# The low part of a stacked operand, formed by GpSimd in two instructions and not by VectorE in one

## The chip, the cores and the metric

One core of a Trainium2 chip runs the whole program. The metric is the device time of one execution in microseconds; a kernel's time is the median of several executions. A core has five engines that run side by side, each with a queue of its own in program order: TensorE (PE, with its weight loads as PEld), VectorE (DVE), ScalarE (ACT), GpSimd (POOL) and SyncE (SP), which issues the transfers here. They wait for each other by semaphores. TensorE's clock has two levels, 1.2 and 2.4 GHz; the profile's granted clock is the share of the higher one.

## The reference

Two layers over 8 sequences of 256 tokens with 1024 features. Cut to what matters:

```python
x = x + L0_ffn(L0_cond(x, w0, itok14), gamma, beta, w1, b1, w3, b3)   # int8 fake-quant feed-forward
# second layer
base  = einsum('bsi,oi->bso', x, weight) + bias
low   = einsum('bsi,bri->bsr', x, lora_a[adapter])                    # rank 16
z     = base + scale[adapter] * einsum('bsr,bor->bso', low, lora_b[adapter])
n     = z * rsqrt(mean(z*z) + eps)
H_res = sinkhorn_50(n @ W_res.T + base_res)      # a 4x4 matrix per token
H_pre, H_post = softmax(n @ W_pre.T + ...), softmax(n @ W_post.T + ...)
x_pre = sum_n(z_streams[n] * H_pre[n])           # 4 streams of 256
out   = x + einsum(H_res, z_streams) + (x_pre @ W_branch) * H_post
```

The products of the second layer run with float32 operands split in two: a rounded high part and a low part, the difference between the full value and the high part. A product is then hi x hi + hi x lo + lo x hi.

## The kernel before

`adaln_ffn` has one block for each engine, and each block is the engine's instructions in program order, so the order on an engine is the order of the Python code. The first layer runs over the sequences `s` and ends, on TensorE, near 460 us. The second layer then runs step `b` = 0 to 7, one sequence of two token tiles (`t` = 0, 1) per step. `b` = 0 has most of its base products woven into the end of the first layer.

**A step on TensorE** (L1042): the base products of tile 0, half 0 (`base`, 24 matmuls L1003), the rank-16 products `low_and_heads` (L991), the transposes of the previous sequence's gathered stream (`branch_transposes`, L1027, which wait on `xp_step` for each tile), base of tile 0, half 1, then `low_rank` (L1011) for both halves, which adds the low-rank term and the bias and waits for `ls_done` and for `e_lo`, then `branch` (L1037), which waits for `xpT_lo`, and the same for tile 1, with the heads and the transposes of the next step's input between.

**The stacked operand.** `low_rank` is one matmul with the stack `ls` (rows 0 to 31 and 32 to 63 the high part of `low`, rows 64 to 95 its low part) against the stack `es` of the adapter's B matrix, the head columns and the bias: `es` holds the high part in rows 0 to 31 and 64 to 95 and the low part in rows 32 to 63. SyncE loads the raw rows three times into `estage` (96 x 1048, float32) and the adapter's scale into `e_scale`; these nine loads wait for the `e_lo` of the step before (`load_lora`, L367). ScalarE writes `es[0:96] = estage * e_scale`, rounded (`stack_hi`, L670, semaphore `e_hi`). VectorE then overwrites rows 32 to 63 with `estage * e_scale - es` in one instruction (L1346, in `lo_stacks`, semaphore `e_lo`), and, in the same function, forms the low part of `ls` (L1349, `ls_done`).

**A step on VectorE** (L1527): `lo_stacks(b)`; `lo_xp(b-1)` (L1417, the low part of the transposed gathered stream); two shares of Sinkhorn iterations; `lo_xT` (L1323) for the next step's tile 0; a third share; `lo_xT` for tile 1; `softmaxes(b)`; `gather(b)`, which forms `xp` of both tiles in two L1399 and six L1405 (`xp = y * hp + xp`); a fourth share. The shares (L1495, L1499, L1502: multiply, reduce, reciprocal) exist in steps 4 to 7 alone. Ahead of step 4 stand `gate_rest` and `sinkhorn_start(0)`, in which VectorE and ScalarE alternate. The iterations of the second half of the tokens follow after step 7.

**A step on ScalarE** (L728): `stack_hi(b)`, the three copies of `evac_ll` (L674 to L676, `f_done`), `evac_xp(b-1)`, the evacuations of `y`, `lora_hi(b+1)` (L664), the high part of the next input, and last `head_root` and `head_exp` of the softmaxes.

**GpSimd** works for the first layer (additions L480 and subtractions L474) and clears the stacks; in the second layer it has one instruction a step, `av_lo` (L496).

Of the kernel before, what the change touches and what calls it, by code (L numbers as in the profile page):

```python
# [9 lines left out]
ALU = mybir.AluOpType  # L10
# [13 lines left out]
def adaln_ffn(nc, x_tok, x_tr, cond_w, ids_cond, ids_lora, gamma, beta, w1, b1, w3, b3, base_w, base_w_nat,  # L24
              lora_a, lora_bt, lora_b_nat, bias_row, bias_col, scaling, head_w, head_base, gate, branch_w, out):
    NB, _, NTOK, D = x_tok.shape
    KC = D // P
    PAIRS = KC // 2
# [26 lines left out]
    def wait(eng, sem, n):  # L55

        if isinstance(n, int) and n <= 0:
            return
        eng.wait_ge(sem, n)

    with ExitStack() as ctx:
# [12 lines left out]
        def sb(name, shape, dt):  # L74
            return sb_in(rest, name, shape, dt)

        def sem(name):
            return ctx.enter_context(nc.semaphore(name))
# [51 lines left out]
        estage = sb("estage", [LZ, D + NH], F32)  # L130
        es = sb("es", [P, D + NH], F32R)
        e_scale = sb("e_scale", [LZ, 1], F32)
# [61 lines left out]

        x1n_ld = [sem(f"x1n_ld{t}") for t in range(NTOK)]
        xt_done, xh_done, xl_done = sem("xt_done"), sem("xh_done"), sem("xl_done")
        a_ld, a_hi, a_lo, e_ld, e_hi, e_lo = sem("a_ld"), sem("a_hi"), sem("a_lo"), sem("e_ld"), sem("e_hi"), sem("e_lo")
        ll_done, f_done, ls_done = sem("ll_done"), sem("f_done"), sem("ls_done")
        l1_done, lg_done, y_ev, ss_done = sem("l1_done"), sem("lg_done"), sem("y_ev"), sem("ss_done")
        hd_step, hd_sqrt, hd_exp, xp_step = sem("hd_step"), sem("hd_sqrt"), sem("hd_exp"), sem("xp_step")  # L200
# [264 lines left out]
        @block.gpsimd  # L465
        def _(pool):
            nc.gpsimd.memset(ident[:, :], 0.0).then_inc(id_zero, 1)
            pool.wait_ge(id_zero, 1)
            nc.gpsimd.affine_select(out=ident[:, :], in_=ident[:, :], compare_op=ALU.not_equal, fill=1.0,
                                    base=0, pattern=[[-1, P]], channel_multiplier=1).then_inc(id_set, 1)  # L470

            def split_lo(pr):
                pool.wait_ge(whi_done, pr + 1)
                nc.gpsimd.tensor_tensor(w_lo[pr][:, :, :], w_raw[pr][:, :, :], w_hi[pr][:, :, :],  # L474
                                        ALU.subtract).then_inc(wlo_done, 1)

            def add_b3(s):
                pool.wait_ge(xr_ld, 16 * (s + 1))
                for t in range(NTOK):
                    nc.gpsimd.tensor_tensor(xres[:, t, :], xres[:, t, :], vecs[:, V_B3, :], ALU.add).then_inc(xb3_done, 1)  # L480

            pool.wait_ge(bias_ld, 16 * 2)
            for s in range(HALF - 2):
                add_b3(s)
            split_lo(0)
            split_lo(1)
            add_b3(HALF - 2)
            split_lo(2)
            split_lo(3)
            for s in range(HALF - 1, NB):  # L490
                add_b3(s)


            def lora_lo(b):
                pool.wait_ge(a_hi, b + 1)
                nc.gpsimd.tensor_tensor(av_lo[:, :, 0:RANK], a_st[:, :, :], av_hi[:, :, 0:RANK],  # L496
                                        ALU.subtract).then_inc(a_lo, 1)

            pool.wait_ge(l0_pair, PAIRS * NB)
            pool.wait_ge(m1_done, 4 * NB)  # L500
            nc.gpsimd.memset(estage[:, :], 0.0)
            nc.gpsimd.memset(e_scale[:, :], 1.0)
            nc.gpsimd.memset(es[:, :].bitcast(F32), 0.0)
            nc.gpsimd.memset(ls[:, :].bitcast(F32), 0.0).then_inc(b_zero, 1)
            pool.wait_ge(b_zero, 1)
            nc.gpsimd.memset(ls[0:32, :].bitcast(F32), 1.0)
            nc.gpsimd.memset(ls[32:64, :].bitcast(F32), 1.0).then_inc(b_set, 1)
            for b in range(NB):
                lora_lo(b)


        @block.scalar
# [667 lines left out]
        def _(dve):  # L1180
# [161 lines left out]


            def lo_stacks(b):
                dve.wait_ge(e_hi, b + 1)
                nc.vector.scalar_tensor_tensor(out=es[32:64, :], in0=estage[32:64, :], scalar=e_scale[32:64, 0:1],  # L1346
                                               in1=es[32:64, :], op0=ALU.mult, op1=ALU.subtract).then_inc(e_lo, 1)
                dve.wait_ge(f_done, b + 1)
                nc.vector.tensor_tensor(ls[LO:LO + RANK, :], PS[0:RANK, LL_BANK, 0:S], ls[0:RANK, :],  # L1349
                                        ALU.subtract).then_inc(ls_done, 1)  # L1350
# [176 lines left out]
            def step_b(b, first=False, last=False, sink=False):  # L1527

                def share(i):
                    if sink:  # L1530
                        n = B_ITERS // 4
                        iterations(0, (b - NB // 2) * B_ITERS + i * n, n)

                lo_stacks(b)
                if not first:
                    lo_xp(b - 1)
                share(0)
                share(1)
                if not last:
                    lo_xT(b + 1, 0)  # L1540
                share(2)
                if not last:
                    lo_xT(b + 1, 1)
                softmaxes(b)
                if not last:
                    gather(b)
                share(3)
# [121 lines left out]
```

## Time and profile before

| | before |
|---|---|
| runs | 820.75, 821.10, 825.47 us; median 821.1 |
| the profiled execution | 823.01 us, span 821.2 us |
| PE busy | 740.1 us, 90% of the span |
| PEld busy | 470.2 us, 57% |
| DVE busy | 528.1 us, 64% |
| ACT busy | 349.4 us, 43% |
| POOL busy | 69.2 us, 8%, 40 instructions |
| chain that ended last | PE 64%, DVE 14%, ACT 11%, DMA 6%, issue 4% |
| granted TensorE clock, mean | 0.965 |

Busy times of different engines overlap. The chain of work that ended last is followed back from the last instruction, at each step to what released it. The idle time in square brackets of a timeline row is what the engine stood still just before the instruction, and behind the arrow is what ended it. Rows of a timeline with x2 or x6 are several instructions, merged; their length is from the start of the first to the end of the last.

### The profile page before, as it was taken

To read this page: it belongs to the slowest core of one execution; us is meant where nothing else is said; L and a number is where in the kernel's file an instruction comes from. 1 tells how busy PE (TensorE), PEld (TensorE's weight loads), DVE (VectorE), ACT (ScalarE), POOL (GpSimd) and SP (SyncE) were. 2 spreads that over 40 slices of the span, in tenths; PEclk is the share of its full clock that TensorE was granted. 3 is DMA by queue.
4 is the path that set the end of the run, shared out by engine and by line. 5 is a ranking of instruction groups with operands and counts; after the bars stand their busy time and mean duration, and the time that the engine had idled before them with its cause. 6 is when DMAs were issued, how large, how long until landed. Compare 5 with 4: busy or idle time off the path is not lost.

```text
span 821.2 us, 9900 instructions
## 1 busy us (share of the span) xinstructions
PE 740.1 (90%) x3112; PEld 470.2 (57%) x3112; DVE 528.1 (64%) x1911; ACT 349.4 (43%) x660; POOL 69.2 (8%) x40
## 2 busy tenths in 40 slices
PE   5977989997989999999999799999899997599927
PEld 2543444353434444444565588888778775367626
DVE  4568254415485756558476445134988988999985
ACT  1234332322443324243455544344454243499714
POOL 0002000201432202002203000000000000000000
PEclk9997999999999999999999999999999999799968
DMA  8978964312545655351303231231230327666406
GB/s 322 405 161 337 242 215 157 137 52 77 208 163 225 262 163 187 103 202 42 113 27 133 86 116 47 70 116 46 71 114 4 116 76 256 217 227 205 150 1 204
DMA packets 54134, 124.31 MB, mean 151 GB/s; under 512 B 7999, under 2 KB 33727, under 8 KB 48450
## 3 DMA queue, kind: packets, MB, share of 16 engines
q1 hardware_dynamic: 52786, 120.94, 42.4%
q10 hardware_dynamic: 1296, 2.74, 1.3%
q8 instruction: 25, 0.41, 0.2%
q14 instruction: 27, 0.22, 0.1%
HBM read 98.47 MB, written 25.19 MB: 151 GB/s over the span
## 4 chain that ended last, share of the span: by engine, by line
PE 64%; DVE 14%; ACT 11%; DMA 6%; issue 4%; SPq 0%; ACTq 0%; DVEq 0%
PE PS L834 21%; PE PS L894 14%; PE PS L1003 13%; PE PS L883 3%; DMA stage<-w_dram 3%; PE PS L1155 2%; DVE xp L1405 2%; PE PS L1115 2%; PE PS L925 2%; ACT blk L783 2%; DMA out_dram<-mr 2%; PE PS L1109 1%; PE PS L1037 1%; ACT qT L561 1%; ACT L690 1%
## 5 line engine op out<-in xcount | busy, mean ns | idle before, releaser
L834 PE MATMUL PS<-w_raw,x_raw 128*128 128x512 f32 x512 | 227.8, 598 | 10.9 <-DMA w_raw<-cond_w_dram 9.6
L834 PEld LDWEIGHTS PS<-w_raw,x_raw 128*128 128x128 f32 x512 | 96.0, 192 | 120.1 <-issue 119.6
L1003 PE MATMUL PS<-w_hi,xT_hi 128*128 128x512 f32 x256 | 102.5, 401 | 0.0
L1003 PE MATMUL PS<-w_hi,xT_lo 128*128 128x512 f32 x256 | 100.1, 391 | 0.0
L1003 PE MATMUL PS<-w_lo,xT_hi 128*128 128x512 f32 x256 | 99.8, 390 | 0.0
L561 ACT ACTIVATE qT<-PS,round_c 128x512 bf16<-128x512 f32 x64 | 40.4, 679 | 76.2 <-PE PS L883 76.2
L1255 DVE SCALAR_TENSOR_TENSOR gbuf<-PS,lnst,vecs 128x512 f32<-128x512 f32 x32 | 23.9, 750 | 75.7 <-PE PS L894 75.7
L480 POOL TENSOR_TENSOR xres<-xres,vecs 128x1024 f32<-128x1024 f32 x16 | 44.0, 2774 | 315.5 <-DMA xres<-x_tok_dram 315.5
L894 PE MATMUL PS<-w3q,qT 128*128 128x512 bf16 x256 | 61.3, 395 | 9.9 <-ACT qT L561 9.9
L1499 DVE TENSOR_REDUCE ksum<-kprod 128x16 f32<-128x64 f32 x392 | 66.4, 211 | 0.0
L894 PE MATMUL PS<-w1q,qT 128*128 128x512 bf16 x256 | 59.6, 387 | 2.2 <-ACT qT L561 2.2
L1323 DVE TENSOR_TENSOR xT_lo<-PS,xT_hi 128x512 fp32r<-128x512 f32 x32 | 20.5, 682 | 62.9 <-ACT xT_hi L621 62.8
L1003 PEld LDWEIGHTS PS<-w_hi,xT_lo 128*128 128x128 f32 x256 | 48.0, 188 | 10.4
L1003 PEld LDWEIGHTS PS<-w_lo,xT_hi 128*128 128x128 f32 x256 | 48.2, 188 | 9.1
L1003 PEld LDWEIGHTS PS<-w_hi,xT_hi 128*128 128x128 f32 x256 | 48.1, 188 | 8.9
L894 PEld LDWEIGHTS PS<-w3q,qT 128*128 128x128 bf16 x256 | 25.1, 101 | 47.6 <-ACT qT L561 14.5
L682 ACT ACTIVATE y<-PS 128x512 f32<-128x512 f32 x32 | 18.2, 598 | 74.5 <-PE PS L1011 74.5
L894 PEld LDWEIGHTS PS<-w1q,qT 128*128 128x128 bf16 x256 | 25.1, 99 | 37.4 <-issue 8.7
L1282 DVE SCALAR_TENSOR_TENSOR x1buf<-PS,q2st,vecs 128x512 f32<-128x512 f32 x32 | 23.6, 750 | 33.0 <-PE PS L894 33.0
L540 ACT ACTIVATE hbuf<-hbuf,round_c,lnst 128x1024 f32<-128x1024 f32 x16 | 19.9, 1241 | 47.9 <-DVE lnst L1242 47.9
L1265 DVE TENSOR_REDUCE q2st<-gbuf 128x1 f32<-128x1024 f32 x16 | 19.5, 1219 | 30.1 <-ACT gbuf L545 30.1
L1502 DVE RECIPROCAL ka<-ksum 128x16 f32<-128x16 f32 x196 | 36.3, 227 | 0.0
(178 smaller groups left out, 1171.4 us busy)
## 6 DMA issues: line engine op xcount, KB each, us to landing
w_raw<-cond_w_dram SPq DMA_DIRECT2D x32, 1024.0 KB, 5.6
x_raw<-x_tr_dram SPq DMA_DIRECT2D x32, 256.0 KB, 6.3
stage<-w_dram SPq DMA_DIRECT2D x16, 512.0 KB, 13.4
xres<-x_tok_dram SPq DMA_DIRECT2D x8, 1024.0 KB, 9.2
x_scratch<-x1buf SPq DMA_DIRECT2D x16, 512.0 KB, 6.3
x1n<-x_scratch SPq DMA_DIRECT2D x16, 512.0 KB, 5.7
y_scratch<-y SPq DMA_DIRECT2D x16, 512.0 KB, 3.4
stage<-base_w_nat_dram SPq DMA_DIRECT2D x8, 512.0 KB, 9.7
```

The costliest lines, as they stand in the source:

```text
L480: nc.gpsimd.tensor_tensor(xres[:, t, :], xres[:, t, :], vecs[:, V_B3, :], ALU.add).then_inc(xb3_done, 1)
L540: nc.scalar.activation(hbuf[t][:, :], hbuf[t][:, :], ACT.Identity, bias=round_c[:, 0:1], scale=lnst[:, t, 9:10]).then_inc(q1_done, 1)
L561: nc.scalar.activation(qT[t][:, 4 * h:4 * h + 4, :], PS[:, T_BANK + h, :].rearrange("p (c n) -> p c n", c=4), ACT.Identity, bias=round_c[: ...
L834: mm = pe.matmul(PS[:, 2 * t + h, :], x_raw[pr][:, c, t * P:(t + 1) * P], w_raw[pr][:, c, h * H2:(h + 1) * H2], start=(pr == 0 and c == 0) ...
L883: tr = pe.transpose(PS[:, T_BANK + h, c * P:(c + 1) * P], src[t][:, (4 * h + c) * P:(4 * h + c + 1) * P], ident[:, :])
L894: mm = pe.matmul(PS[:, O_BANK + h, :], qT[t][:, c, :], wq[:, c, h * H2:(h + 1) * H2], start=(c == 0), stop=(c == KC - 1))
L1003: pe.matmul(PS[:, 2 * t + h, :], xx[:, c, t * P:(t + 1) * P], ws[c // 2][:, c % 2, h * H2:(h + 1) * H2], start=(c == 0 and xx is xT_hi and ...
L1255: nc.vector.scalar_tensor_tensor(out=g[:, h * H2:(h + 1) * H2], in0=PS[:, O_BANK + h, :], scalar=lnst[:, t, 8:9], in1=vecs[:, V_SW1, h * H ...
L1282: nc.vector.scalar_tensor_tensor(out=x1buf[t][:, h * H2:(h + 1) * H2], in0=PS[:, O_BANK + h, :], scalar=q2st[:, t, 1:2], in1=vecs[:, V_SW3 ...
L1323: nc.vector.tensor_tensor(xT_lo[:, 4 * h:4 * h + 4, t * P:(t + 1) * P], PS[:, T_BANK + h, :].rearrange("p (c n) -> p c n", c=4), xT_hi[:, ...
L1499: nc.vector.tensor_reduce(ksum[i][:, :, :], kprod[i][:, :, :, :], AX.X, ALU.add).then_inc(k_step[i], 1)
L1502: nc.vector.reciprocal(new[i][:, :, :], ksum[i][:, :, :]).then_inc(k_step[i], 1)
```

## The change

VectorE's L1346 goes. GpSimd gets a function `stack_lo(b)` with two instructions over rows 32 to 63: `estage = estage * e_scale`, in place, and, after a semaphore of its own, `es = estage - es`, which signals `e_lo` as L1346 did. GpSimd runs `stack_lo(b)` between `lora_lo(b)` and `lora_lo(b+1)`, and `lora_lo` gets a wait for the `e_lo` of the step before. The other engines wait for the same semaphores as before.

```diff
-        a_ld, a_hi, a_lo, e_ld, e_hi, e_lo = sem("a_ld"), sem("a_hi"), sem("a_lo"), sem("e_ld"), sem("e_hi"), sem("e_lo")
+        a_ld, a_hi, a_lo, e_ld, e_hi, e_scaled, e_lo = sem("a_ld"), sem("a_hi"), sem("a_lo"), sem("e_ld"), sem("e_hi"), sem("e_scaled"), sem("e_lo")
...
             def lora_lo(b):
+                wait(pool, e_lo, b)
                 pool.wait_ge(a_hi, b + 1)
...
+            def stack_lo(b):
+                pool.wait_ge(a_lo, b + 1)
+                pool.wait_ge(e_hi, b + 1)
+                nc.gpsimd.tensor_scalar(estage[32:64, :], estage[32:64, :], e_scale[32:64, 0:1], None, ALU.mult).then_inc(e_scaled, 1)
+                pool.wait_ge(e_scaled, b + 1)
+                nc.gpsimd.tensor_tensor(es[32:64, :], estage[32:64, :], es[32:64, :], ALU.subtract).then_inc(e_lo, 1)
+
+            lora_lo(0)
             for b in range(NB):
-                lora_lo(b)
+                stack_lo(b)
+                if b + 1 < NB:
+                    lora_lo(b + 1)
...
             def lo_stacks(b):
-                dve.wait_ge(e_hi, b + 1)
-                nc.vector.scalar_tensor_tensor(out=es[32:64, :], in0=estage[32:64, :], scalar=e_scale[32:64, 0:1],
-                                               in1=es[32:64, :], op0=ALU.mult, op1=ALU.subtract).then_inc(e_lo, 1)
                 dve.wait_ge(f_done, b + 1)
```

GpSimd's queue at the end of its memsets, where the second layer starts, before:

```order
L504 MEMSET ls 128x256
L506 MEMSET ls 32x256
L507 MEMSET ls 32x256
L496 TENSOR_TENSOR av_lo<-a_st,av_hi 128x8x16 x8
L61 UNCONDITIONAL_BRANCH
```

and after the change, where the code stands one line further down:

```order
L505 MEMSET ls 128x256
L507 MEMSET ls 32x256
L508 MEMSET ls 32x256
L497 TENSOR_TENSOR av_lo<-a_st,av_hi 128x8x16
L512 TENSOR_SCALAR estage<-estage,e_scale 32x1048
L514 TENSOR_TENSOR es<-estage,es 32x1048
L497 TENSOR_TENSOR av_lo<-a_st,av_hi 128x8x16
L512 TENSOR_SCALAR estage<-estage,e_scale 32x1048
L514 TENSOR_TENSOR es<-estage,es 32x1048
```

The eight `av_lo` stood in a row and now have a scaling and a subtraction behind each of them.

VectorE's queue where step 5 ends its predecessor's fourth share and begins, before:

```order
L1499 TENSOR_REDUCE ksum<-kprod 128x16 x2
L1502 RECIPROCAL kb<-ksum 128x16 x2
L1346 SCALAR_TENSOR_TENSOR es<-estage,e_scale,es 32x1048
L1349 TENSOR_TENSOR ls<-PS,ls 16x256
L1417 TENSOR_TENSOR xpT_lo<-PS,xpT_hi 128x512
L1495 TENSOR_TENSOR kprod<-kmat,kb 128x64 x2
```

and after it (L1510 was L1502, L1357 was L1349, L1425 was L1417, L1503 was L1495):

```order
L1507 TENSOR_REDUCE ksum<-kprod 128x16 x2
L1510 RECIPROCAL kb<-ksum 128x16 x2
L1357 TENSOR_TENSOR ls<-PS,ls 16x256
L1425 TENSOR_TENSOR xpT_lo<-PS,xpT_hi 128x512
L1503 TENSOR_TENSOR kprod<-kmat,kb 128x64 x2
```

The low part of `ls` follows directly on the last reciprocal; nothing else moved on VectorE.

## Rows read from the trace of the kernel before

**Rows 1.** Chain that ended last, in time: start us, length us, engine, out, line
```profile
477.22 1.99 DVE xp L1405 x5
...
480.09 5.48 PE PS L1003 x24
...
611.46 1.30 DVE es L1346
...
782.89 12.42 issue
```

**Rows 2.** Timelines of step 5, ScalarE, VectorE, TensorE: start us, us, instruction, idle before
```profile
602.80 1.16 ACT L670 ACTIVATE es<-estage,e_scale 96x1048 fp32r<-96x1048 f32 x1
...
604.09 2.46 DVE L1405 SCALAR_TENSOR_TENSOR xp<-y,hp,xp 128x256 f32<-128x256 f32 x6
...
611.46 1.30 DVE L1346 SCALAR_TENSOR_TENSOR es<-estage,e_scale,es 32x1048 fp32r<-32x1048 f32 x1
...
612.79 0.41 DVE L1349 TENSOR_TENSOR ls<-PS,ls 16x256 fp32r<-16x256 f32 x1
...
613.24 0.69 DVE L1417 TENSOR_TENSOR xpT_lo<-PS,xpT_hi 128x512 fp32r<-128x512 f32 x1
...
606.21 0.83 PE L1027 MATMUL PS<-ident,xp 128*128 128x128 f32 x4 [0.45 <-DVE xp L1405]
...
612.13 0.39 PE L1003 MATMUL PS<-w_hi,xT_lo 128*128 128x512 f32 x1
...
613.26 0.72 PE L1011 MATMUL PS<-es,ls 128*128 128x512 f32 x2 [0.74 <-DVE ls L1349]
...
614.08 0.35 PE L1037 MATMUL PS<-wb_hi,xpT_hi 128*128 128x256 f32 x1
```

**Rows 3.** Instructions that touch es: duration ns min/median/max, first and last start
```profile
L1346 DVE SCALAR_TENSOR_TENSOR es<-estage,e_scale,es x8: 1298/1298/1300, 462.1 to 675.7; 32x1048 fp32r<-32x1048 f32 x8
```

**Rows 4.** Timelines of GpSimd and VectorE, two places of the first layer
```profile
248.48 4.50 POOL L474 TENSOR_TENSOR w_lo<-w_raw,w_hi 128x2048 fp32r<-128x2048 f32 x1 [10.85 <-ACT w_hi L517]
...
248.62 5.45 DVE L1287 TENSOR_TENSOR x1buf<-x1buf,xres 128x1024 f32<-128x1024 f32 x1
...
73.91 5.64 POOL L480 TENSOR_TENSOR xres<-xres,vecs 128x1024 f32<-128x1024 f32 x2 [72.42 <-DMA xres<-x_tok_dram]
...
74.10 3.24 DVE L1259 TENSOR_TENSOR gbuf<-gbuf,vecs 128x1024 f32<-128x1024 f32 x1
```

**Rows 5.** Timeline of GpSimd, the short subtraction of step 4
```profile
584.57 0.46 POOL L496 TENSOR_TENSOR av_lo<-a_st,av_hi 128x128 fp32r<-128x128 f32 x1 [33.69 <-ACT av_hi L664]
```

**Rows 6.** Timelines of VectorE and GpSimd, the memsets ahead of the second layer
```profile
446.08 1.23 DVE L1259 TENSOR_TENSOR gbuf<-gbuf,vecs 128x1024 f32<-128x1024 f32 x1
...
446.32 0.97 POOL L503 MEMSET es<- 128x1048 f32 x1
```

**Rows 7.** Timelines of ScalarE and VectorE, step 2
```profile
506.64 1.16 ACT L670 ACTIVATE es<-estage,e_scale 96x1048 fp32r<-96x1048 f32 x1
...
507.92 2.46 DVE L1405 SCALAR_TENSOR_TENSOR xp<-y,hp,xp 128x256 f32<-128x256 f32 x6
```

**Rows 8.** Timelines of ScalarE and TensorE: step 4, then two gaps of the first layer
```profile
576.45 1.16 ACT L670 ACTIVATE es<-estage,e_scale 96x1048 fp32r<-96x1048 f32 x1
...
580.01 1.22 PE L1011 MATMUL PS<-es,ls 128*128 128x512 f32 x2 [2.10 <-DVE ls L1349]
...
231.29 5.31 PE L894 MATMUL PS<-w3q,qT 128*128 128x512 bf16 x16 [2.37 <-ACT qT L561]
...
371.16 3.63 PE L894 MATMUL PS<-w3q,qT 128*128 128x512 bf16 x16 [1.03 <-ACT qT L561]
```

**Rows 9.** TensorE by stretch: length, PE busy, granted clock, DMA share, GB/s
```profile
581.00:582.00 1.00, 1.00 (x6) 0.50 0.04 2
```

**Rows 10.** Timelines of ScalarE and TensorE, step 0
```profile
457.83 1.17 ACT L670 ACTIVATE es<-estage,e_scale 96x1048 fp32r<-96x1048 f32 x1 [2.95 <-DMA e_scale<-scaling_dram]
...
465.06 1.20 PE L1011 MATMUL PS<-es,ls 128*128 128x512 f32 x4 [1.56 <-DVE ls L1349]
```

## The prediction

> **What bounds the kernel now.** I read the chain of waits first, then the engine timelines of one step of the second layer, then every place where GpSimd and VectorE work at the same time. The steps run from about 470 to 692 us. In them the chain is TensorE's, but in each step it passes through one VectorE group: in steps 1 to 3 only through the gather `xp` (L1405), in steps 5 to 7 through the gather and then through `es` L1346, the instruction that goes away [rows 1]. After 692 us VectorE's Sinkhorn iterations bound it; TensorE waits 12.42 us near the end for them [rows 1]. So what moves the end of step 7 moves the end of the program by as much: VectorE and TensorE can start nothing of the tail's first part before TensorE has ended step 7.
>
> Step 5 shows how tight it is [rows 2]. TensorE waits 0.45 us for the gather before the transposes L1027. It issues a product every 0.23 us (24 in 5.48 [rows 1]), so after the last L1003 at 612.13 it could take the low-rank product L1011 at 612.36. It starts it at 613.26, because VectorE runs L1346 and L1349 up to 613.20, and L1037 starts at 614.08 and not at 612.36 + 0.46 = 612.82. VectorE costs TensorE 614.08 - 612.82 = 1.26 us there; the views of steps 6 and 7 read alike, with the same 1.30 us of L1346 on the chain.
>
> **What is removed.** Eight L1346 of 1.30 us [rows 3]. In steps 0 to 3 L1346 is not on the path: in steps 1 to 3 the chain shows the gather alone. In steps 5 to 7 taking 1.33 us (with its gap) out of VectorE brings `ls` to 611.87, before TensorE's 612.36, and `xpT_lo` to 612.60, before 612.82. Gain 1.26 us a step, **-3.8 us** for three steps.
>
> **What is added.** Sixteen GpSimd instructions over 32 partitions and 1048 columns. No row has these shapes. For the subtraction, the rows are 4.50 us for 2048 columns [rows 4] and 0.46 us for 128 [rows 5]: 2.10 ns a column, so 0.46 + 920 x 0.0021 = 2.40 us. For the scaling, the bounds are a memset of the same 1048 columns, 0.97 us [rows 6], and the 2.40 us of a two-input instruction. I take 1.1: it reads one stream and writes one, so it lies near the memset. The Trainium skill ("GPSIMD Engine Reference", section 3 on performance against the Vector engine) gives about 1.03 cycles an element at 1.2 GHz for a simple one-input body, which would be 0.9 us and a start on top, by which the sum would not change; no run here shows it.
>
> As a wait this is covered in most steps. GpSimd starts when `es` hi is ready (L670 ends at 603.96), so by itself `e_lo` is there near 607.7, 4.6 us before TensorE could use it [rows 2]. Queued behind the pair on GpSimd is the next step's `av_lo`; it needs ScalarE's `av_hi`, which comes only after the low-rank products, so it isn't held up. Queued behind `e_lo` on SyncE are the next step's nine operand loads, which could only leave earlier.
>
> **The port.** The cost is elsewhere. Where a GpSimd instruction that reads SBUF runs, a VectorE instruction with two SBUF inputs stands still until it is over. L1287, 1.23 us alone, took 5.45 us beside a 4.50 us subtraction that had begun 0.14 us earlier: 4.22 us lost. L1259 took 3.24 us beside a GpSimd pair, and that pair, two of 2.27, took 5.64: they took turns, the whole of one after the whole of the other [rows 4]. Beside a memset, which only writes, L1259 kept its 1.23 us [rows 6].
>
> The new pair starts at the worst moment. In step 5 `es` hi ends at 603.96 and the gather's six L1405 (each reads `y` and `xp`, both in SBUF) begin at 604.09. In step 2 it is 507.80 and 507.92 [rows 2, 7]; steps 3, 6 and 7 have the same 0.1 us. So the scaling falls on the first or second L1405 and the subtraction, after its semaphore, on the next but one. TensorE's L1027 needs the fifth. VectorE loses about 1.0 + 2.2 = 3.2 us (each instruction less some 0.14 us of start-up), and L1027 comes 3.2 us later. In step 1 `es` hi ends inside the gather, with three or four L1405 left; I still count 3.2.
>
> TensorE then stands idle 0.45 + 3.2 = 3.65 us in each of these steps. After an idle 2.37 us sixteen L894 took 5.31 us, after 1.03 us 3.63. After an idle 2.10 us, ended at 580.01, the granted clock is 0.50, the lower of its two levels (1.2 of 2.4 GHz) [rows 8, 9]. So each such step loses another 5.31 - 3.63 = 1.7 us.
>
> **The sum.** Steps 1 to 3: 3.2 + 1.7 = 4.9 us each, nothing given back: **+14.7**. Steps 5 to 7: 4.9 - 1.3 = 3.6 each, **+10.8**; with TensorE now ready at 612.36 + 4.9 = 617.3 and `ls` at 611.87 + 3.2 = 615.1, VectorE is not waited for a second time. Step 4 is different: there the gather is over long before `es` hi, which ends at 577.61 behind the exponentials, and nothing covers the new pair. 577.7 + 1.1 + 0.2 + 2.4 = 581.4 against L1011 at 580.01 [rows 8]; with turns lost to VectorE's two-input L1478 and L1481 I take 581.6, **+1.6**. Its clock fall is there already. Step 0: `es` hi ends at 459.00 and TensorE waits for `ls` until 465.06 [rows 10]; 459.1 + 3.7, and even a turn more, ends before that; nothing. Together 14.7 + 10.8 + 1.6 = +27.1. The profiled execution took 823.0 us (span 821.2), which gives 850.1; it lay 1.9 us above the median of the runs, so **848 us** on the median of 821.1.
>
> **The rivals.**
> - Only the subtraction holds VectorE up (no row has a one-input GpSimd instruction that reads beside such work). Stall 2.2, idle 2.65, the clock still falls: 3 x 3.9 + 3 x 2.6 + 1.6 = 21, **842**. The scaling does read SBUF, as those that held did. The Trainium skill ("SBUF — State Buffer", "Who interferes with whom") has any GpSimd instruction that reads SBUF contend with a two-input VectorE one; for the subtraction the trace agrees (4.22 us), for the scaling no run here shows it.
> - The clock holds through these gaps. 3 x 3.2 + 3 x 1.9 + 1.6 = 17, **838**. Against it: the gaps of 2.10 and 2.37 us did bring it down.
> - GpSimd's subtraction doesn't get in between the six L1405, which start every 0.4 us, and waits until the gather is over. Then L1027 comes only 1.0 us later, without a fall of the clock, and the subtraction runs against the iterations' two-input L1495 instead: of 2.2 us some 1.7 are lost, since 0.5 of each 0.8 us is single-input work. Steps 1 to 3 +1.0, steps 5 to 7 -1.3 + 1.0 + 1.6, step 4 +1.6: +8.5, **830**. No row shows back-to-back two-input work beside a waiting GpSimd; the turns of [rows 4] speak against it.
> - The scaling costs as much as the subtraction, 2.40: 1.3 more in six steps, **856**.
> - On the other side: 32 partitions do not stop VectorE, or not for long. The place is the gather. Then -3.8 + 1.6 gives **819**, no change that can be told. It decides at a stall d of 6d + 1.6 - 3.8 = 0, 0.37 us a step. All colliding rows have 128 partitions, which leaves it room; nothing in them suggests that the lock looks at partitions.
>
> **How the numbers follow.** Likeliest case 0.56, then 0.12, 0.10, 0.11, 0.06 and 0.05 in the order above. About 1% (8 us) is what a measurement of this kernel can tell from no change. Slower by more: the first case, 842, 838, 856 and two thirds of 830, some 0.88. Within 1%: 0.10. No case gives 8 us; I leave 0.02. The range takes in 838 to 856 with a little below for shorter instructions: 836 to 856. Left out are 830 and 819, 0.16.
>
> **What the profile after would show.** Right: the six L1405 of steps 1 to 3 and 5 to 7 take 5 to 6 us and not 2.46; L1027 waits more than 3 us for `xp` in six steps; the clock is at half for some 3 us behind it; the first low-rank product waits for `e_lo` in step 4 alone; steps 1 to 3 near 35.6 us apart. Wrong: L1405 keeps 2.46 us (the 819 case), or L1495 in the share behind the gather is stretched (830), or gaps without a slow clock (838). A GpSimd subtraction well off 2.4 us moves every case by six times the difference.

## The result and the profile after

| | before | after |
|---|---|---|
| runs | 6, median 823.49 us (820.75 to 825.60) | 6, median 834.65 us (833.42 to 836.12) |
| ratio of the medians | | 1.0143, 95% interval 1.0116 to 1.0169 |
| the profiled execution | 823.01 us, span 821.2 us | 833.84 us, span 831.8 us |
| granted clock, mean | 0.965 | 0.964 |

The change makes the kernel slower by 1.4%, 11.2 us on the medians and 10.6 us between the two spans. The sign was forecast, with a size of 27 us.

Busy time of the engines after, and the chain that ended last by engine:

```profile
PE 739.7 (89%) x3112; PEld 470.4 (57%) x3112; DVE 530.2 (64%) x1903; ACT 349.5 (42%) x660; POOL 114.0 (14%) x56
...
PE 63%; DVE 18%; ACT 9%; DMA 4%; issue 4%; POOL 1%; SPq 0%; ACTq 0%; DVEq 0%; POOLq 0%
```

GpSimd has sixteen instructions more and is busy for 44.8 us more, 5.6 us a step where the prediction counted 3.5. VectorE lost eight instructions of 1.30 us, 10.4 us, and is still 2.1 us busier than before: something stretched its other work by 12.5 us. Six gathers held for 0.80 us each and three pairs of the iterations held for 2.00, both read below, make 10.8 of it. GpSimd stands on the chain with only 1%.

The two new instructions over the eight steps (duration in ns, shortest, median, longest):

```profile
L512 POOL TENSOR_SCALAR estage<-estage,e_scale x8: 2941/3276/3561, 459.4 to 677.7; 32x1048 f32<-32x1048 f32 x8
...
L514 POOL TENSOR_TENSOR es<-estage,es x8: 2381/2448/2460, 462.4 to 681.3; 32x1048 fp32r<-32x1048 f32 x8
```

The subtraction has the predicted length. The scaling takes 2.9 to 3.6 us and not 1.1: the instruction with one input is the longer of the two.

Step 5 of after (L1413 is the gather, L1405 before; L1503 was L1495; L1038, L1022 and L1048 were L1027, L1011 and L1037), to be held against [rows 2]:

```profile
609.19 1.16 ACT L681 ACTIVATE es<-estage,e_scale 96x1048 fp32r<-96x1048 f32 x1
...
610.48 3.25 DVE L1413 SCALAR_TENSOR_TENSOR xp<-y,hp,xp 128x256 f32<-128x256 f32 x6
613.65 0.35 DVE L1503 TENSOR_TENSOR kprod<-kmat,kb 128x64 f32<-128x64 f32 x2
...
614.46 2.35 DVE L1503 TENSOR_TENSOR kprod<-kmat_t,ka 128x64 f32<-128x64 f32 x2
...
620.64 0.42 DVE L1357 TENSOR_TENSOR ls<-PS,ls 16x256 fp32r<-16x256 f32 x1
...
610.87 3.20 POOL L512 TENSOR_SCALAR estage<-estage,e_scale 32x1048 f32<-32x1048 f32 x1 [19.59 <-ACT es L681]
614.15 2.44 POOL L514 TENSOR_TENSOR es<-estage,es 32x1048 fp32r<-32x1048 f32 x1
...
613.39 0.83 PE L1038 MATMUL PS<-ident,xp 128*128 128x128 f32 x4 [1.24 <-DVE xp L1413]
...
621.11 0.72 PE L1022 MATMUL PS<-es,ls 128*128 128x512 f32 x2 [1.41 <-DVE ls L1357]
...
621.92 0.36 PE L1048 MATMUL PS<-wb_hi,xpT_hi 128*128 128x256 f32 x1
```

The gather takes 3.25 us and not 2.46: the scaling held it for 0.8 us, though it ran from 610.87 to past the gather's end. The gather is over at 613.73, and only at 614.15 does the subtraction start. So the subtraction meets the Sinkhorn iterations: one pair of L1503 takes 2.35 us where its neighbour takes 0.35, 2.00 us lost. The gap before the transposes is 1.24 us (0.45 before), and behind it L1038 takes the same 0.83 us as before; the gap of 3.65 us and the slow clock that were forecast are absent. TensorE waits again before L1022, 1.41 us where it was 0.74: VectorE comes to `ls` later by 0.80 + 2.00 - 1.33 = 1.47 us, TensorE itself by the gather's 0.80 alone.

In steps 1 to 3 no iteration stands behind the gather, and only the 0.8 us is left. Step 2, to be held against [rows 7]:

```profile
508.91 3.26 DVE L1413 SCALAR_TENSOR_TENSOR xp<-y,hp,xp 128x256 f32<-128x256 f32 x6
...
511.83 0.83 PE L1038 MATMUL PS<-ident,xp 128*128 128x128 f32 x4 [1.25 <-DVE xp L1413]
```

In step 4 the pair lies on the path. Its place in the chain of waits (start us, length us, engine, out, line):

```profile
580.37 3.04 POOL estage L512
583.48 2.39 POOL es L514
586.01 1.19 PE PS L1022 x2
```

and TensorE's first wait there, against 2.10 us in [rows 8]:

```profile
586.01 1.19 PE L1022 MATMUL PS<-es,ls 128*128 128x512 f32 x2 [5.50 <-POOL es L514]
```

**Where the 10.6 us go.** The start of the branch product (L1037 before, L1048 after) in steps 1 to 7 measures what each step adds:

| step | 1 | 2 | 3 | 4 | 5 | 6 | 7 |
|---|---|---|---|---|---|---|---|
| before, us | 485.87 | 516.66 | 547.43 | 581.03 | 614.08 | 646.18 | 678.29 |
| after, us | 486.85 | 518.43 | 550.01 | 587.00 | 621.92 | 655.51 | 689.11 |
| later by | 0.98 | 1.77 | 2.58 | 5.97 | 7.84 | 9.33 | 10.82 |
| added in the step | 0.79 + 0.19 | 0.79 | 0.81 | 3.39 | 1.87 | 1.49 | 1.49 |

The 0.19 us is there before the pair first runs (ScalarE's first `es` starts at 457.83 before and 458.02 after; the first L1011 of step 0 at 465.06, its L1022 at 465.25). Steps 1 to 3 add the stall of the gather. Step 4 adds what its pair takes beyond the wait that was there. A step of 5 to 7 adds 0.80 + 2.00 - 1.33 = 1.47 us: both stalls less the removed VectorE instruction and its gap; 1.49 measured. In step 5 another 0.38 us comes from the clock behind step 4's gap, which was at 0.50 until 590. It isn't shown that this 0.38 us comes from the longer gap: in `after_gather` the gap of step 4 is as long (5.53 us) and the slow stretch behind it costs no more than in before, and in `late3_8` it is before's 2.10 us and costs 0.4 us more. The rows (length, PE busy, ..., granted clock, DMA share, GB/s):

```profile
588.00:590.00 2.00, 2.00 (x11) 1.90 (x10) 2.00 (x16) 1.28 (x3) 0.00 (x0) 0.50 0.14 33
590.00:592.00 2.00, 2.00 (x10) 1.66 (x9) 2.00 (x17) 0.59 (x2) 0.54 (x1) 0.95 0.18 34
```

### The profile page after: what moved, and what is told of

Its sections match the earlier page's. It is cut to its first block, busy times and chain, and to the rows that moved or that the text cites. A ratio compares the mean times of both kernels' runs of the same rounds, so it can differ in the third digit from the quotient of the medians.

```text
span 831.8 us, 9923 instructions
## 1 busy us (share of the span) xinstructions
PE 739.7 (89%) x3112; PEld 470.4 (57%) x3112; DVE 530.2 (64%) x1903; ACT 349.5 (42%) x660; POOL 114.0 (14%) x56
## 4 chain that ended last, share of the span: by engine, by line
PE 63%; DVE 18%; ACT 9%; DMA 4%; issue 4%; POOL 1%; SPq 0%; ACTq 0%; DVEq 0%; POOLq 0%
PE PS L845 19%; PE PS L1014 13%; PE PS L905 13%; DVE xp L1413 3%; DMA stage<-w_dram 3%; PE PS L894 3%; PE PS L1126 2%; PE PS L1120 2%; DVE kprod L1503 2%; PE PS L1166 2%; PE PS L936 2%; PE PS L1048 2%; PE PS L1135 1%; DVE ksum L1507 1%; ACT qT L572 1%
## 5 line engine op out<-in xcount | busy, mean ns | idle before, releaser
L845 PE MATMUL PS<-w_raw,x_raw 128*128 128x512 f32 x512 | 227.8, 598 | 11.2 <-DMA w_raw<-cond_w_dram 9.8
L512 POOL TENSOR_SCALAR estage<-estage,e_scale 32x1048 f32<-32x1048 f32 x8 | 26.4, 3296 | 134.6 <-ACT es L681 134.6
L1503 DVE TENSOR_TENSOR kprod<-kmat_t,ka 128x64 f32<-128x64 f32 x196 | 40.6, 249 | 0.0
```

The costliest lines, as they stand in the source:

```text
L512: nc.gpsimd.tensor_scalar(estage[32:64, :], estage[32:64, :], e_scale[32:64, 0:1], None, ALU.mult).then_inc(e_scaled, 1)
L845: mm = pe.matmul(PS[:, 2 * t + h, :], x_raw[pr][:, c, t * P:(t + 1) * P], w_raw[pr][:, c, h * H2:(h + 1) * H2], start=(pr == 0 and c == 0) ...
L1503: nc.vector.tensor_tensor(kprod[i][:, :, :, :], (kmat if row else kmat_t)[i][:, :, :, :], cols(v, HG), ALU.mult).then_inc(k_step[i], 1)
```

## The experiments

The theory after the result (A): the scaling of 3 us holds VectorE for 0.8 us only, the subtraction for some 2 us wherever it starts, it gets in between any two VectorE instructions, and the scaling's length decides where that is. The rival (B) was the one of the prediction in which GpSimd does not get in between back-to-back L1405. Diffs are against the changed kernel. Medians of before were 823.09 us (13 runs) beside the first four kernels and 823.85 us (25 runs) beside the other four. The first branch product of step 1 starts anywhere from 485.8 to 490.5 us in the profiles, mostly because of what lies before the second layer's steps (the first low-rank product of step 0 starts between 463.9 and 468.2), so beside each median stands the **stretch**: from the first branch product of step 1 to that of step 7. It leaves out what step 1 itself loses, 0.79 us in after. It is 192.42 us in before and 202.26 us in after.

| kernel | median, us (runs) | ratio, 95% interval | stretch, us |
|---|---|---|---|
| `neither` | 816.58 (4) | 0.9912, 0.9885 to 0.9940 | 186.54 |
| `sub_only` | 841.62 (4) | 1.0219, 1.0190 to 1.0248 | 205.81 |
| `scale_only` | 824.41 (10) | 1.0011, 0.9990 to 1.0032 | 191.97 |
| `after_gather` | 832.07 (4) | 1.0102, 1.0067 to 1.0136 | 199.37 |
| `ahead` | 816.98 (8) | 0.9918, 0.9890 to 0.9947 | 186.01 |
| `step4_dve` | 832.02 (10) | 1.0092, 1.0063 to 1.0120 | 198.52 |
| `late3_8` | 822.42 (10) | 0.9988, 0.9963 to 1.0013 | 192.24 |
| `forms` | 833.54 (1) | | 200.85 |

### neither: what the removal alone is worth

```diff
-                nc.gpsimd.tensor_scalar(estage[32:64, :], estage[32:64, :], e_scale[32:64, 0:1], None, ALU.mult).then_inc(e_scaled, 1)
-                pool.wait_ge(e_scaled, b + 1)
-                nc.gpsimd.tensor_tensor(es[32:64, :], estage[32:64, :], es[32:64, :], ALU.subtract).then_inc(e_lo, 1)
+                nc.gpsimd.memset(es[32:64, 0:1].bitcast(F32), 0.0).then_inc(e_lo, 1)
```

> GpSimd's scaling and subtraction are left out; a memset of one column, which signals e_lo, stands in their place, so the low rows of the operand are wrong. Theory (the two instructions cost through the read port and through e_lo in step 4, nothing else does): VectorE loses L1346 and nothing is held. Steps 5 to 7 gain 1.26 us each, step 4 starts its low-rank product at 579.0 instead of 580.0 and its idle gap shrinks from 2.1 to about 1.1 us, so its fall of the clock (1.7 us) may go too. Together 3.8 + 1.0 + 1.7 = 6.5 us under the kernel before, about 817. Rival (the moved wait and the semaphores on GpSimd's queue cost by themselves): no faster than the kernel before.

Measured: 816.58 us, 6.5 us under before. The branch products of steps 5 to 7 are 30.78 us apart where before's are 32.11: 1.33 us given back in each, the length of the removed instruction. Step 4 gives the rest. TensorE's wait there falls from 2.10 to 1.11 us, and the clock doesn't fall behind it:

```profile
579.04 0.73 PE L1020 MATMUL PS<-es,ls 128*128 128x512 f32 x2 [1.11 <-DVE ls L1355]
```

Two L1020 take 0.73 us here, 1.22 us in [rows 8]. So the removal had more to give than the 3.8 us counted, and in step 4 it could not be had with the pair on GpSimd.

### sub_only: the subtraction straight into the gather

```diff
-                nc.gpsimd.tensor_scalar(estage[32:64, :], estage[32:64, :], e_scale[32:64, 0:1], None, ALU.mult).then_inc(e_scaled, 1)
-                pool.wait_ge(e_scaled, b + 1)
                 nc.gpsimd.tensor_tensor(es[32:64, :], estage[32:64, :], es[32:64, :], ALU.subtract).then_inc(e_lo, 1)
```

> The scaling is left out, the subtraction stays and starts straight after e_hi; the low rows are wrong. Theory A, the working on record: the subtraction gets in between the six gather instructions, holds them 2.2 us, TensorE is idle 2.65 us before the transposes and its clock falls. Steps 1 to 3 +3.9 us each, steps 5 to 7 +2.6, step 4 about 0: 19.5 us over the kernel before, 843, and so slower than the changed kernel, although it has less work. Theory B (GpSimd does not get a turn between back-to-back two-input instructions and waits for the gather's end): steps 1 to 3 nothing, steps 5 to 7 +0.7 us each, about 825.6, and the gather keeps 2.46 us.

Measured: 841.62 us; A said 843. Less work than the changed kernel, and 7.0 us slower than it. The stretch shows 3.55 us of that, and most of the rest is step 1's own stall: from the first low-rank product of step 0 to the first branch product of step 1 it is 24.51 us here, 21.60 in after and 20.81 in before. Step 1, then step 2:

```profile
477.16 4.60 DVE L1411 SCALAR_TENSOR_TENSOR xp<-y,hp,xp 128x256 f32<-128x256 f32 x6
...
478.15 2.54 POOL L512 TENSOR_TENSOR es<-estage,es 32x1048 fp32r<-32x1048 f32 x1 [9.46 <-ACT es L679]
...
511.66 4.71 DVE L1411 SCALAR_TENSOR_TENSOR xp<-y,hp,xp 128x256 f32<-128x256 f32 x6
...
511.68 2.44 POOL L512 TENSOR_TENSOR es<-estage,es 32x1048 fp32r<-32x1048 f32 x1 [18.55 <-ACT es L679]
...
516.03 1.09 PE L1036 MATMUL PS<-ident,xp 128*128 128x128 f32 x4 [2.70 <-DVE xp L1411]
```

```profile
516.00:518.00 2.00, 1.97 (x7) 1.58 (x8) 1.00 (x3) 0.60 (x1) 0.00 (x0) 0.61 0.60 242
518.00:520.00 2.00, 2.00 (x6) 1.54 (x6) 0.48 (x1) 0.00 (x0) 0.00 (x0) 0.53 0.99 322
```

In step 2 the subtraction starts 0.02 us after the first L1411 and stretches the six of them by 2.25 us, its own 2.44 less 0.19. TensorE's gap becomes 2.70 us and the clock behind it is near its lower level. This is the picture that was predicted. By itself step 2 could be a matter of who came first, but in step 1 the subtraction starts 0.99 us into the gather: the first three L1411 took 0.48 us each, the fourth 2.63. That refutes rival B: GpSimd does get in between instructions that follow each other without a gap. The run also shows that in the changed kernel the scaling protects the gather, by keeping the subtraction back until the gather is over. Step 5 differs in one thing: behind its gap of 2.68 us the granted clock stayed at 1.00.

### scale_only: the scaling alone

```diff
-                nc.gpsimd.tensor_scalar(estage[32:64, :], estage[32:64, :], e_scale[32:64, 0:1], None, ALU.mult).then_inc(e_scaled, 1)
-                pool.wait_ge(e_scaled, b + 1)
-                nc.gpsimd.tensor_tensor(es[32:64, :], estage[32:64, :], es[32:64, :], ALU.subtract).then_inc(e_lo, 1)
+                nc.gpsimd.tensor_scalar(estage[32:64, :], estage[32:64, :], e_scale[32:64, 0:1], None, ALU.mult).then_inc(e_lo, 1)
```

> The subtraction is left out, the scaling signals e_lo; the low rows are wrong. Theory (the scaling takes 3.0 us but holds the gather only 0.8): gather 3.26 us in steps 1 to 3 and 5 to 7, +0.8 us in each of steps 1 to 3, -0.5 in each of steps 5 to 7 (TensorE then waits at the transposes and no longer at ls), step 4 +0.8 since e_lo comes at 580.8: 2.4 - 1.4 + 0.8 = 1.8 us over the kernel before, 825. Rival (the scaling costs what its length says, 3 us a step): 6 x 3.0 - 3.8 + 0.8 = 15 us over it, 838.

Measured: 824.41 us, where A said 825 and the rival 838. Step 2, then TensorE in step 4:

```profile
511.52 3.25 DVE L1411 SCALAR_TENSOR_TENSOR xp<-y,hp,xp 128x256 f32<-128x256 f32 x6
...
511.56 3.56 POOL L512 TENSOR_SCALAR estage<-estage,e_scale 32x1048 f32<-32x1048 f32 x1 [18.22 <-ACT es L679]
...
586.15 0.70 PE L1020 MATMUL PS<-es,ls 128*128 128x512 f32 x2 [3.04 <-POOL estage L512]
```

A 3.56 us instruction ran under the whole of the gather and cost it 0.79 us. The gap of 1.24 us behind it left the clock alone. So did the gap of 3.04 us in step 4, where the granted clock stayed at 1.00 and the two low-rank products took 0.70 us, not the 1.22 of [rows 8].

### after_gather: the pair held back until the gather is over

```diff
                 pool.wait_ge(e_hi, b + 1)
+                wait(pool, xp_step, 8 * b)
                 nc.gpsimd.tensor_scalar(estage[32:64, :], estage[32:64, :], e_scale[32:64, 0:1], None, ALU.mult).then_inc(e_scaled, 1)
```

> The changed kernel, whose pair in addition waits for the end of the gather (xp_step at 8b). Nothing is left out. Theory: steps 1 to 3 lose nothing, since VectorE has no two-input work there and e_lo (479.7 + 3.0 + 2.4 = 485.1) is just there for 485.4; in steps 5 to 7 both instructions run against the iterations: 0.5 + 2.0 - 1.3 = +1.2 us each; step 4 keeps its 3.8. Together 3.6 + 3.8 = 7.4 us over the kernel before, 831, and 3.5 us under the changed kernel. Rival (the place within a step doesn't matter, only the length of GpSimd's work): as the changed kernel, 834.7.

Measured: 832.07 us; in the stretch 2.9 us better than after. The gather is back at 2.46 us, and both instructions now meet the iterations in step 5:

```profile
607.53 2.46 DVE L1414 SCALAR_TENSOR_TENSOR xp<-y,hp,xp 128x256 f32<-128x256 f32 x6
...
610.73 1.16 DVE L1504 TENSOR_TENSOR kprod<-kmat_t,ka 128x64 f32<-128x64 f32 x2
...
613.97 2.27 DVE L1504 TENSOR_TENSOR kprod<-kmat,kb 128x64 f32<-128x64 f32 x2
...
618.09 0.73 PE L1023 MATMUL PS<-es,ls 128*128 128x512 f32 x2 [2.13 <-DVE ls L1358]
```

1.16 and 2.27 in place of 0.35 twice: 0.81 us to the scaling, 1.92 us to the subtraction. The two holds are the same at another place and against another instruction. In steps 6 and 7 the multiply began 0.54 us into the scaling and lost only 0.44 to 0.46 us: it pays for what is left of the hold. Steps 1 to 3 cost next to nothing any more (30.88 us apart where before's are 30.79). Step 4 keeps its loss (3.37 us). Of the 1.87 + 1.49 + 1.49 us that after added in steps 5 to 7, 1.34 + 1.03 + 1.03 are left.

### step4_dve: step 4's low part back on VectorE

```diff
             def stack_lo(b):
+                if b == 4:
+                    return
...
             def lo_stacks(b):
+                if b == 4:
+                    dve.wait_ge(e_hi, b + 1)
+                    nc.vector.scalar_tensor_tensor(out=es[32:64, :], in0=estage[32:64, :], scalar=e_scale[32:64, 0:1],
+                                                   in1=es[32:64, :], op0=ALU.mult, op1=ALU.subtract).then_inc(e_lo, 1)
```

> The changed kernel with step 4's low part left to VectorE's single instruction. Nothing is left out. Theory: step 4 alone gives back its share, 5.97 - 2.58 = 3.4 us between the branch products of steps 3 and 4, and 0.4 us of the slow clock in step 5: 830.9. Rival (the late e_lo in step 4 is hidden by the idle TensorE there anyway): 834.7.

Measured: 832.02 us, and the stretch is 3.74 us shorter than that of after. TensorE's wait in step 4 is before's again:

```profile
586.29 1.22 PE L1024 MATMUL PS<-es,ls 128*128 128x512 f32 x2 [2.10 <-DVE ls L1363]
```

So in these profiles step 4 alone carries 3.7 us of the 10.6: 3.39 us in it, and 0.36 us in step 5, about what after's slower clock cost there. The medians point the same way (8.2 us over before, where the changed kernel is 11.2).

### late3_8: eight short subtractions behind the gather, steps 5 to 7 alone

```diff
+                wait(pool, xp_step, 8 * b)
+                cuts = range(0, D + NH, (D + NH) // 8)
+                for c in cuts:
+                    ins = nc.gpsimd.tensor_tensor(es[32:64, c:c + cuts.step], estage[32:64, c:c + cuts.step],
+                                                  es[32:64, c:c + cuts.step], ALU.subtract)
...
+                if b >= 5:
+                    act.wait_ge(e_hi, b + 1)
+                    nc.scalar.activation(estage[32:64, :], estage[32:64, :], ACT.Copy, scale=e_scale[32:64, 0:1]).then_inc(e_scaled, 1)
```

> Steps 0 to 4 by VectorE as before; in steps 5 to 7 ScalarE writes the scaled rows in full precision (its idle 1.8 us ahead of the copies of ls) and GpSimd subtracts in eight pieces of 131 columns behind the gather. Nothing is left out. Theory: a piece takes 0.46 us, holds VectorE at most that long and often falls on single-input work: 0.06 to 0.24 us each as av_lo does, so 0.5 to 1.9 us a step against the 1.33 taken away: between -2.5 and +1.7 us in all, likeliest 0, 823. Rival (pieces hold as long in sum as one subtraction, 2.0 us): +0.7 a step, 825.5.

Measured: 822.42 us, no difference from before. The question was whether the hold is paid for each piece or for each moment in which VectorE wants the port. In step 5:

```profile
609.96 3.43 POOL L517 TENSOR_TENSOR es<-estage,es 32x131 fp32r<-32x131 f32 x8 [22.46 <-DVE xp L1425]
...
610.52 0.84 DVE L1515 TENSOR_TENSOR kprod<-kmat_t,ka 128x64 f32<-128x64 f32 x2
...
611.81 0.81 DVE L1515 TENSOR_TENSOR kprod<-kmat,kb 128x64 f32<-128x64 f32 x2
...
613.08 0.52 DVE L1515 TENSOR_TENSOR kprod<-kmat_t,ka 128x64 f32<-128x64 f32 x2
```

0.49 + 0.46 + 0.17 = 1.12 us lost in place of 2.00: three multiplies got through while the eight pieces ran, and the reductions and reciprocals between them kept their length (0.33 to 0.37 us), so a piece that falls on one of these costs nothing. In steps 6 and 7 that leaves 31.9 us between branch products, 0.2 less than before's 32.1. What is still lost is about what the 1.33 us of the removed instruction give back, and the stretch is 192.24 us against 192.42.

### forms: what sets the scaling's length

```diff
+                n = (1048, 524, 1048, 1048, 524, 1048, 128, 524)[b]
+                s = 2.0 if b in (0, 2, 7) else e_scale[32:64, 0:1]
+                nc.gpsimd.tensor_scalar(estage[32:64, 0:n], estage[32:64, 0:n], s, None, ALU.mult).then_inc(e_scaled, 1)
```

> The changed kernel with other forms of the scaling in steps 0 to 7: 1048, 524, 1048, 1048, 524, 1048, 128, 524 columns; steps 0, 2 and 7 multiply by a constant 2.0 and not by the scale's column, so the low rows are wrong. A look at single instructions. Theory A (the scalar from SBUF is not what makes it slow): the constant's form takes 2.9 us at 1048 columns too, and lengths and holds go with the columns: 524 about 1.5 us with 0.4 held. Theory B (the pointer is what is slow): the constant's form takes about 1.1 us, as the working on record had it. In steps 1, 6 and 7 the scaling is short enough that the subtraction falls within the gather again: gather 4.7 us and more there and TensorE's clock at half behind it; in steps 2, 3 and 5 under theory A as in the changed kernel.

Measured, one execution. Step 0, with a constant in place of the scale's column, beside a VectorE addition that began 0.66 us into it and lost 0.24; then step 4, half the columns with the column of scales:

```profile
462.05 2.86 POOL L514 TENSOR_SCALAR estage<-estage 32x1048 f32<-32x1048 f32 x1 [4.21 <-ACT es L683]
...
582.19 1.67 POOL L514 TENSOR_SCALAR estage<-estage,e_scale 32x524 f32<-32x524 f32 x1 [26.84 <-ACT es L683]
```

A constant is as slow as a column of scales (2.86 us, and 2.94 us in step 0 of after), so fetching the scale isn't what takes the time. The length follows the columns: (2.94 - 1.67) / 524 = 2.4 ns a column, or 2.6 with the 3.03 us of step 4 in after. The hold falls with them too. In step 1, with 524 columns, the gather took 2.82 us, a hold of 0.36; there the subtraction started 0.3 us after the gather's end, so that part of the expectation missed. Behind a shorter scaling the subtraction does start inside the gather, as the prediction had it (step 6 with 128 columns, then step 7 with 524 columns and a constant):

```profile
643.92 4.63 DVE L1415 SCALAR_TENSOR_TENSOR xp<-y,hp,xp 128x256 f32<-128x256 f32 x6
...
643.96 1.22 POOL L514 TENSOR_SCALAR estage<-estage,e_scale 32x128 f32<-32x128 f32 x1 [18.89 <-ACT es L683]
645.27 2.60 POOL L516 TENSOR_TENSOR es<-estage,es 32x1048 fp32r<-32x1048 f32 x1
...
676.87 5.00 DVE L1415 SCALAR_TENSOR_TENSOR xp<-y,hp,xp 128x256 f32<-128x256 f32 x6
```

What this costs hangs on the clock. In step 6 it held behind a gap of 2.61 us, and the step took 33.04 us, less than the 33.59 of after: a stall in the gather spares the iterations. In step 7 it fell, and the step took 34.70 us against 33.60.

### ahead: the operand formed one step earlier, all on ScalarE and VectorE

`neither` shows what there is to be had: some 6 us, if VectorE's instruction and step 4's wait go away. This kernel gets it with the whole computation and without GpSimd. A second buffer lets ScalarE write the high part of step b+1 in step b, and VectorE forms the low part where it would wait for ScalarE's root in the softmaxes.

```diff
-        es = sb("es", [P, D + NH], F32R)
+        es2 = [sb(f"es{i}", [P, D + NH], F32R) for i in range(2)]
...
                     evac_xT(b + 1, 0)
+                    stack_hi(b + 1)
...
                 n[0] += 1
+                if b + 1 < NB:
+                    stack_lo(b + 1)
                 dve.wait_ge(hd_sqrt, b + 1)
```

Here `stack_lo(b)` is before's one instruction on VectorE with its wait for `e_hi`, and it is called for step 0 at its old place.

> The kernel before with a second buffer for the operand es: ScalarE writes the high part of step b+1 in step b, ahead of the last evacuation of y, and VectorE runs its single instruction for step b+1 in the 1.35 us in which it waits for the square root of step b's softmaxes. Nothing is left out and GpSimd does nothing new. Theory: L1346 (1.30 us) fits the gap, so VectorE loses nothing where TensorE waits for it; steps 5 to 7 gain 1.26 us each, and step 4 gains what the run without both instructions gained there, since ScalarE no longer writes es between the exponentials and ls. As that run: 816.5, 6.5 us under the kernel before. Rival (the gap is worth nothing because the square root's successors start late by the instruction's tail): 1 to 2 us back, 818 to 819.

Measured: 816.98 us (815.73 to 819.49), 0.8% under before and 2.1% under the changed kernel. Step 5, the instruction in its new place:

```profile
592.45 1.16 ACT L671 ACTIVATE es<-estage,e_scale 96x1048 fp32r<-96x1048 f32 x1
...
600.24 0.17 DVE L1370 TENSOR_SCALAR hd<-hd 128x2 f32<-128x2 f32 x1 [0.23 <-ACT sq L687]
600.44 1.30 DVE L1349 SCALAR_TENSOR_TENSOR es<-estage,e_scale,es 32x1048 fp32r<-32x1048 f32 x1
601.77 0.17 DVE L1375 RECIPROCAL hd<-hd 128x2 f32<-128x2 f32 x1
```

The reciprocal that needs the root follows at once, and the stretch is 186.01 us, against 186.54 in `neither`; the rival's 1 to 2 us aren't there. In after the same reciprocal of a later step (L1374 at 640.71) waited 1.34 us for that root, as long as the instruction takes, so it is free here. In step 4 the operand is long ready, and TensorE waits 0.76 us:

```profile
582.18 0.74 PE L1014 MATMUL PS<-es,ls 128*128 128x512 f32 x2 [0.76 <-DVE ls L1356]
```

## Why the prediction was wrong

**The step that failed: the scaling's price and its hold.** The prediction took 1.1 us for the scaling, near the memset's 0.97 ("it reads one stream and writes one"), and let it hold VectorE for all of it. Both halves are wrong. It measures 2.94 us in step 0 and up to 3.56 us beside the gather, which lies outside both bounds (0.97 and 2.40): the row of a memset says nothing on an instruction that computes. And it holds VectorE for 0.8 us of its 3. In step 0 of after, two VectorE instructions with two inputs ran inside the scaling at their full speed:

```profile
459.37 2.94 POOL L512 TENSOR_SCALAR estage<-estage,e_scale 32x1048 f32<-32x1048 f32 x1 [3.77 <-ACT es L681]
...
460.47 1.23 DVE L1298 TENSOR_TENSOR x1buf<-x1buf,xres 128x1024 f32<-128x1024 f32 x1
461.61 0.69 DVE L1445 TENSOR_TENSOR wb_lo<-wbst,wb_hi 128x512 fp32r<-128x512 f32 x1
```

The first began 1.10 us into the scaling and took the 1.23 us of [rows 6]. So by then the hold was over. In step 5's gather the third L1413 began 0.40 us into the scaling and took 1.27 us where the first two took 0.48 each, so the hold ended there about 1.2 us in. In step 2 the third began 0.75 us into a longer scaling (3.56 us, where step 5's took 3.20) and the hold ended 1.55 us in. Both times, and in steps 1 and 3 as well, the hold ended 2.0 us before the scaling did: what makes a scaling longer beside the gather lies ahead of that. The rule was carried over from rows in which GpSimd's instructions had two inputs [rows 4]. The Trainium skill ("SBUF — State Buffer", "Who interferes with whom") has any GpSimd instruction that reads SBUF contend with a two-input VectorE one. The traces agree that the scaling contends, and show it holding VectorE for 0.8 us of its 2.9 to 3.6. The Trainium skill ("GPSIMD Engine Reference", section 3) gives the 1.03 cycles an element that the prediction cites as the bound that the ports set, and 1.8 as the best case. The 2.4 ns a column measured here are 2.9 cycles at 1.2 GHz, above both, so a duration could not be had from the bound.

**What hung on it.** With 1.1 us the subtraction would have started some 1.2 us behind `es` hi, in the middle of the gather. With 3.0 to 3.3 us it starts 0.4 us after the gather's end. The forecast stall of 3.2 us in the gather became 0.8; TensorE's gap became 1.24 and not 3.65 us; the clock did not fall. Steps 1 to 3 add 0.8 us each and not 4.9, 12.3 us less in all. Steps 5 to 7 add 0.8 + 2.0 - 1.33 and not 3.6, 6.4 us less in all, though there the subtraction hurts all the same, at the iterations. Step 4 adds 3.8 and not 1.6. 27.1 - 12.3 - 6.4 + 2.2 = 10.6 us, which is the difference of the spans.

**Point by point.**
- *The chain and the tail.* Right. The first branch product of step 7 came 10.82 us later, the span is 10.6 us longer.
- *The removal gives 1.26 us a step in steps 5 to 7.* Right (1.33 in `neither`), but step 4 was taken for lost: "its clock fall is there already". In `neither` its wait is 1.11 us and the clock holds, a gain of 5.88 - 3 x 1.33 = 1.9 us in the stretch that can't be had while the pair ends last there.
- *The subtraction, 2.40 us, holding 2.2.* Right: 2.38 to 2.46 us, and 2.25, 2.00 and 1.92 us lost in `sub_only`, after and `after_gather`.
- *GpSimd takes its turn between L1405 that follow each other.* Right (step 1 of `sub_only`; steps 6 and 7 of `forms`).
- *The clock falls behind a gap like that.* Right in five of the six steps in which the gap arose in `sub_only`; in step 5 the clock held behind 2.68 us. There are two more such cases, below, so a fall behind every gap of this size was too sure.
- *Step 4, +1.6 us.* Mis-sized by the same term. `es` hi to `e_lo` was put at 4.0 us (577.6 to 581.6); it takes 580.19 to 585.87, 5.7 us. Against before that is +3.4 us, and 0.4 more with the slow clock in step 5. `step4_dve` shows 3.7.
- *Step 0 and the loads.* Right that they cost nothing. That the loads "could only leave earlier" was wrong, though: in step 2 `e_lo` came at 515.04 us, 3.3 us later than before's 511.71. The loads left at 516.55, behind another load in the queue, as before's did at 514.60.
- *The arithmetic.* A longer scaling would have added its 1.3 us in step 4 too, so 857 and not 856; and the chances of "slower by more" add up to 0.91, not 0.88. Neither matters for the outcome.

**The rivals.** 830 came nearest (+8.5), and described the trace well in the steps: 1.0 us in the gather, the subtraction against the iterations, no fall of the clock. But its reason, that GpSimd does not get in between the L1405, is refuted. It had been the only case in which the subtraction falls behind the gather; that it might do so because the scaling is long was not asked. The rival with a longer scaling, 856, was worked out with the lock for its whole length, and so got the wrong sign: with the scaling in place the kernel is faster than without it (834.65 against 841.62 in `sub_only`), and the steps that gain are mainly 1 to 3, where nothing behind the gather can be held.

**What stays open.** What the scaling does in its last 2 us isn't shown; that it reads early and computes and writes later would fit, but no run separates the two. That a scaling grows from 2.94 to 3.56 us because it first waits for its turn at the port would fit the constant 2.0 us behind the hold, but isn't shown either. Why the clock falls behind one gap and holds behind a longer one is open as well.

## What to carry to other kernels

Before pricing contention with GpSimd, get a length for each instruction and, apart from it, how long it holds the other engine; an instruction without a row of its own kind needs bounds as wide as the difference between a memset and three times that. Where two instructions follow each other, the first one's length decides what the second one meets: work out the outcome for both ends of that length, since here the longer first instruction was the better one, above all in the steps with nothing to hold behind the gather. If work is to leave a busy engine, look first for a wait in that engine's own queue that can take it, one step ahead with a second buffer: that gave 0.8%, where moving it to GpSimd cost 1.4%.

## What the runs showed of the hardware that was not expected

- A GpSimd multiplication by a scalar over 32 x 1048 float32 takes 2.94 us, more than the subtraction of two operands of the same shape (2.38 us), and a constant is as slow as a column of scales (2.86 us). Half the columns take 1.67 us.
- Its hold on VectorE is a part of it, and shrinks with the columns: 0.80 us for 1048, 0.36 us for 524, 0.03 us for 128. In the gathers of after it ended 2.0 us before the scaling did, whether that took 3.17 or 3.56 us. The subtraction's hold is nearly its whole length, 2.25 of 2.44 us.
- A subtraction on 32 partitions holds VectorE nearly as long as it runs (2.25 of 2.44 us), as the one on 128 partitions did (4.22 of 4.50 [rows 4]).
- Gap and clock don't go together simply. Behind a gap of 2.10 us in step 4 [rows 8, 9] and of 2.70 us in `sub_only` the granted clock fell. In step 6 of `forms` TensorE stood still for 2.61 us and the clock held; in step 7, after 2.98 us, it fell. It held too after 3.04 us in step 4 of `scale_only` and after 2.68 us in step 5 of `sub_only`. The first two rows are TensorE's timeline in `forms`, the last two its granted clock behind the gaps:

```profile
648.21 0.83 PE L1040 MATMUL PS<-ident,xp 128*128 128x128 f32 x4 [2.61 <-DVE xp L1415]
...
681.53 1.11 PE L1040 MATMUL PS<-ident,xp 128*128 128x128 f32 x4 [2.98 <-DVE xp L1415]
```

```profile
650.00:652.00 2.00, 2.00 (x10) 1.63 (x9) 2.00 (x17) 0.00 (x0) 0.00 (x0) 1.00 1.02 334
...
682.00:684.00 2.00, 2.00 (x8) 1.71 (x7) 2.00 (x17) 0.60 (x1) 0.00 (x0) 0.50 0.85 340
```
